# A fused cross-attention, self-attention and 8-bit feed-forward kernel: w_down's rounding and turning moved into the self-attention groups, three banks for gate and up, and two borders reordered

## The reference

```python
x = x + cross_attention(layernorm(x), ctx, Wq, Wk, Wv, Wo, bo)      # 64 x 32 tokens of 512, 257 keys of 384, 16 heads of 64
x = x + self_attention(layernorm(x), Wq, Wk, Wv, Wo, rel_bias_emb)  # per batch of 32 tokens, bias by bucket
x = x + ffn(layernorm(x), clip_x, clip_down, w_gate, w_up, w_down)  # hidden width 1408

def _act_fake_quant(x, clip):                                        # one scale for the whole tensor
    scale = sigmoid(clip) * max(abs(x)) / 127
    return clip(round(x / scale), -128, 127) * scale
def _weight_fake_quant(w):                                           # one scale for each row
    scale = max(abs(w), axis=1, keepdims=True) / 127
    return clip(round(w / scale), -128, 127) * scale
xq = _act_fake_quant(x, clip_x)
h = _act_fake_quant(silu(xq @ wq(w_gate).T) * (xq @ wq(w_up).T), clip_down)
out = h @ wq(w_down).T
```

## Time and profile before

| | us |
|---|---|
| median of 3 runs | 1700.52 (1699.65 to 1701.18) |
| the profiled execution | 1699.84 |
| its span | 1698.1 |
| PE busy | 1602.0 (94%) |
| DVE busy | 1105.7 (65%) |
| ACT busy | 776.6 (46%) |
| POOL busy | 299.0 (18%) |

### The profile page before, as it was taken

How to read it: one execution, slowest core, us unless ns; L and a number is a source line. 1 busy time by engine, 2 the same in 40 slices (tenths; PEclk the granted TensorE clock), 3 DMA queues, 4 the chain that set the end, 5 groups by cost and what they waited for, 6 DMA issues and landing times.

```text
span 1698.1 us, 33888 instructions
## 1 busy us (share of the span) xinstructions
PE 1602.0 (94%) x12487; PEld 1327.5 (78%) x12487; DVE 1105.7 (65%) x2297; ACT 776.6 (46%) x1687; POOL 299.0 (18%) x179
## 2 busy tenths in 40 slices
PE   5999879999999999999999998899999999986888
PEld 4888668898998999989999897778778787763333
DVE  6776666667666766667666676457565565566886
ACT  3555554555545555455554554232122221214555
POOL 0000123222232222323222231100000000002325
PEclk9999989999999999999999999999999999998989
DMA  4898842332133312333123331320202202040032
GB/s 165 324 372 331 321 169 103 114 124 69 73 114 114 124 59 83 114 114 123 48 94 114 114 120 47 102 106 26 100 33 66 85 32 76 33 179 26 32 117 99
DMA packets 68445, 197.82 MB, mean 116 GB/s; under 512 B 4560, under 2 KB 21008, under 8 KB 65552
## 3 DMA queue, kind: packets, MB, share of 16 engines
q1 hardware_dynamic: 68368, 196.73, 31.3%
HBM read 127.77 MB, written 68.94 MB: 116 GB/s over the span
## 4 chain that ended last, share of the span: by engine, by line
PE 61%; issue 28%; DVE 6%; DMA 2%; ACT 2%; POOL 1%; SPq 0%; ACTq 0%; POOLq 0%; DVEq 0%
PE psum_o L641 16%; PE psum_s L610 12%; PE psum_o L656 5%; PE psum_q L669 5%; PE psum_o L522 5%; PE psum_q L610 4%; PE psum_t L621 3%; PE psum_t L581 2%; PE psum_o L1739 2%; PE psum_s L1739 2%; PE psum_q L628 1%; PE psum_t L538 1%; DMA c_raw<-in_ctx_dram 1%; PE psum_q L538 1%; PE psum_s L538 1%
## 5 line engine op out<-in xcount | busy, mean ns | idle before, releaser
L641 PE MATMUL psum_o<-pT,c_nat 128*128 128x512 f32 x1152 | 314.0, 410 | 8.5 <-DVE pT L890 5.2
L610 PE MATMUL psum_s<-cT,qk 128*128 128x258 f32 x1728 | 254.1, 291 | 10.1 <-ACT probs L825 5.3
L610 PEld LDWEIGHTS psum_s<-cT,qk 128*128 128x128 f32 x1728 | 226.9, 191 | 21.4 <-issue 6.2
L641 PEld LDWEIGHTS psum_o<-pT,c_nat 128*128 128x128 f32 x1152 | 207.0, 193 | 45.6 <-DVE pT L890 7.4
L1160 POOL TENSOR_TENSOR c_nat<-c_raw,zero 128x768 fp32r<-128x768 f32 x64 | 95.4, 1491 | 805.7 <-PE psum_o L641 603.4
L825 ACT ACTIVATE probs<-psum_s,nmax 128x257 f32<-128x257 f32 x192 | 91.7, 478 | 222.9 <-DVE nmax L1064 222.7
L1048 DVE SCALAR_TENSOR_TENSOR oT<-p_last,c_last,psum_o 128x512 f32<-128x512 f32 x192 | 142.8, 744 | 72.7 <-PE psum_o L641 70.4
L890 DVE TENSOR_TENSOR pT<-psum_t,pT 128x512 fp32r<-128x512 f32 x128 | 87.7, 686 | 72.5 <-ACT pT L721 72.5
L1163 POOL TENSOR_TENSOR c_nat<-c_raw,c_nat 128x768 fp32r<-128x768 f32 x64 | 122.2, 1910 | 5.0
L721 ACT ACTIVATE cT<-psum_t 128x256 fp32r<-128x256 f32 x192 | 67.3, 388 | 114.4 <-PE psum_t L581 114.3
L1064 DVE TENSOR_REDUCE nmax<-psum_s 128x1 f32<-128x257 f32 x192 | 80.8, 421 | 50.7 <-PE psum_s L610 49.7
(11 more groups left out here) (241 smaller groups left out, 3076.4 us busy)
## 6 DMA issues: line engine op xcount, KB each, us to landing
qk_by_tile<-staged SPq DMA_DIRECT2D x32, 1536.0 KB, 9.9
raw<-qk_by_tile SPq DMA_DIRECT2D x16, 3072.0 KB, 10.6
c_raw<-in_ctx_dram SPq DMA_DIRECT2D x64, 384.0 KB, 3.2
out_dram<-x_out SPq DMA_DIRECT2D x32, 256.0 KB, 2.0
x_in<-in_x_dram SPq DMA_DIRECT2D x4, 1024.0 KB, 5.7
x_res<-in_x_dram SPq DMA_DIRECT2D x16, 256.0 KB, 2.7
x_in<-out_dram SPq DMA_DIRECT2D x4, 1024.0 KB, 7.2
x_res<-out_dram SPq DMA_DIRECT2D x16, 256.0 KB, 2.8
```

Of the source, the lines that this page charges most:

```text
L610: m = pe.matmul(ps[:, 0:SKP], qk[:, part, rg, c, b, :], cT[b % 2][:, moving, c, :], start=(c, part, moving) == (0, 0, 0), stop=(c, part) = ...
L641: i = pe.matmul(ps[:], c_nat[(b - 1) % 2][:, part, k, m * P:(m + 1) * P], pT[:, moving, k, :], start=(k, part, moving) == (0, 0, 0), stop= ...
```

## The change

w_down is prepared like gate/up chunks: chunks 11 to 14 are its four blocks of 128 rows of 1408. There are now 15 chunks, 3, 4, 4, 4 a group, at j = 2, 4, 6, 7, so all of w_down's fall into the last group. The DVE finds scale and clamp (down_scale, filled here), the ACT rounds, the PE transposes 8 and 3 blocks to t1 and t0, the DVE copies, SP stores to wd_dram; wdT is loaded back before wguT. The buffers w_stage, wd_stage, w_nat, wd_nat, w_turned now lie over v2_1, so the ACT waits for the group's last store before it writes v of tile 1 (it waited before aT of tile 0). wdT is [P, KD, FC, P]: a down product reads 512 columns in four runs. From the gate and up turns the steps of w_down are gone on all engines, and the POOL has only the two reductions and the last adds. Gate products use s0, s1, t0, up products o0, o1, t1, with four silu buffers. The row product (ROW) and the sd_wide copy are made before the first turn. At the border to self-attention w2q_low moves ahead of x_out. In the last group: rsqrt of tiles 0 and 1 after x_out of tile 1; aT of tile 3 ahead of the norm of tiles 0 and 1; rsqrt of tile 2; after the last x_out rsqrt of tile 3 and the norm of tiles 2 and 3. w2o_low moves from j = 7 to 6, and turned banks are emptied ahead of the next chunk's scaling. The ACT waits for the last x_out store before it rounds x, since the silu buffers lie over x_out4.

The diff, cut to what the prediction speaks of:

```diff
@@ self_units, gate_up_units, down_units @@
+CHUNK_AT = (2, 4, 6, 7)
-            if j in (3, 5, 7) and (j - 3) // 2 < group_chunks[s]:
-                u.append((("GUT", chunk), "t1"))
+            if j in CHUNK_AT and CHUNK_AT.index(j) < group_chunks[s]:
+                u += [(("GUT", chunk), "t1")] if chunk < 11 else [(("DT", chunk - 11, 0), "t1"), (("DT", chunk - 11, 1), "t0")]
-    u = [((w, i), (("s0", "s1"), ("o0", "o1"))[w == "U"][i % 2]) for i in range(11) for w in "GU"]
-    return u + [(("DT", 0), "t0"), (("DT", 1), "t1")] + (x_units() if not last else [])
+    u = [((w, i), (("s0", "s1", "t0"), ("o0", "o1", "t1"))[w == "U"][i % 3]) for i in range(11) for w in "GU"]
+    return u + (x_units() if not last else [])
...
-        CHUNKS = (2, 3, 3, 3)
+        CHUNKS = (3, 4, 4, 4)
@@ dve_cross_tile @@
                     dve_qk_low(dve, t + 1, 3, section)
+                if not more and b == 3:
+                    dve_weight(dve, "q")
                 if b == 3 and begun:
                     dve_x_out(dve, t, section)
...
-                if not more and b == 3:
-                    dve_weight(dve, "q")
@@ act_self_all @@
                 act_exp(act, s, 0)
+                act.wait_ge(s_wgu, 16 * sum(CHUNKS[:s + 1]))
                 act_self_v(act, s, 1, 0)
...
-                act.wait_ge(s_wgu, 16 * sum(CHUNKS[:s + 1]))
                 act_self_attended(act, s, 0)
@@ dve_gate_up_weights @@
+            if c >= FC:
+                n = c - FC
+                dve.wait_ge(s_down_raw, 16 * n + 16)
+                ch.link(V.tensor_reduce(wrow[:, 0:1], wd_stage[:], AX_X, ALU.max, apply_absolute_value=True))
+                ch.link(V.tensor_scalar(wrow[:, 2:3], wrow[:, 0:1], 1.0 / 127.0, None, ALU.mult))
+                ch.step(V.tensor_scalar(down_scale[:, n:n + 1], wrow[:, 2:3], 1.0, None, ALU.mult))
+                ch.link(V.reciprocal(wrow[:, 4:5], wrow[:, 2:3]))
+                clamp(wd_stage[:], wrow[:, 4:5], wd_stage[:], ch.link).then_inc(s_dclamp, 1)
+                return
@@ dve_self_all @@
                 dve_self_out(dve, s, 1, ch2)
+                if not more:
+                    dve_out_rsqrt(dve, slice(0, 2), ch2)
                 dve_self_attended(dve, s, 2)
...
                 dve_self_out(dve, s, 2, ch2)
+                dve_self_attended(dve, s, 3)
                 if not more:
-                    dve_out_norm(dve, s, slice(0, 3), ch2)
-                dve_self_attended(dve, s, 3)
+                    dve_out_norm(dve, s, slice(0, 2), ch2)
+                    dve_out_rsqrt(dve, slice(2, 3), ch2)
                 dve_self_out(dve, s, 3, ch2)
                 if not more:
-                    dve_out_norm(dve, s, slice(3, 4), ch2)
+                    dve_out_rsqrt(dve, slice(3, 4), ch2)
+                    dve_out_norm(dve, s, slice(2, 4), ch2)
@@ pe_gate_up @@
-                if i == 10:
-
-                    pe.wait_ge(s_dround, n + 1)
...
-                        m.then_inc(done, 1)
@@ pe_ffn @@
-            pe.wait_ge(s_wguback, 16)
+            pe.wait_ge(s_wide, 1)
+            ps, done = empty(pe, U3(("ROW",), 0, "first"))
+            for c in range(KD):
+                m = pe.matmul(ps[:, c * P:(c + 1) * P], sd_wide[:, c, :], ident[:], start=True, stop=True)
+            m.then_inc(done, 1)
+            pe.wait_ge(s_wguback, 32)
...
-                        out_ = pe.matmul(ps[:], hq[n % 2][:, i, m * P:(m + 1) * P], wdT[:, i, :], start=i == 0,
+                        out_ = pe.matmul(ps[:], hq[n % 2][:, i, m * P:(m + 1) * P], wdT[:, :, i, :], start=i == 0,
@@ dve_gate_up @@
-                if i == 0:
-                    dve_down_scales(dve, n, ch)
-                if i == 2:
-                    V.tensor_scalar(wd_stage[:], wd_stage[:], down[:, 2:3], 127.0, ALU.mult, ALU.min).then_inc(s_dclamp, 1)
@@ pool_ffn @@
-            with pool.Fori(0, NCH) as n:
...
-                G.tensor_scalar(wd_nat[:], wd_stage[:], -ROUND, None, ALU.add).then_inc(s_dround, 1)
```

More of the change, by code:

```diff
@@ L863, in act_cross_tile @@
                 act_last_scalars(act, b, 4 * t)
+                if b == 3 and not more:
+                    act_weight(act, "q")
                 if b == 3 and more:
@@ L1363, in pe_turn_weights @@
             pe.wait_ge(s_wround, c + 1)
+            if c >= FC:
+                for part, chunks in enumerate((range(8), range(8, FC))):
+                    ps, done = empty(pe, own(("DT", c - FC, part)))
+                    for k in chunks:
+                        m = pe.transpose(bf16_blocks(ps, 2 * D)[:, k % 8, :], wd_nat[:, k * P:(k + 1) * P], ident16[:])
+                    m.then_inc(done, 1)
+                return
             ps, done = empty(pe, own(("GUT", c)))
@@ L1434, in act_round_weights @@
         def act_round_weights(act, c):
-            act.wait_ge(s_wclamp, 2 * c + 2)
-            if c:
+            if c > FC:
+                for part in range(2):
+                    full(act, own(("DT", c - FC - 1, part)))
+            elif c:
                 full(act, own(("GUT", c - 1)))
-            nc.scalar.activation(w_nat[:], w_stage[:], ACT.Copy, bias=-ROUND).then_inc(s_wround, 1)
+            if c < FC:
+                act.wait_ge(s_wclamp, 2 * c + 2)
+                nc.scalar.activation(w_nat[:], w_stage[:], ACT.Copy, bias=-ROUND).then_inc(s_wround, 1)
+            else:
+                act.wait_ge(s_dclamp, c - FC + 1)
+                nc.scalar.activation(wd_nat[:], wd_stage[:], ACT.Copy, bias=-ROUND).then_inc(s_wround, 1)
         def halves(ap):
@@ L1759, in pe_ffn @@
             pe_gate_up(pe, NCH - 1, "last")
-            pe.wait_ge(s_wide, 1)
-            ps, done = empty(pe, U3(("ROW",), 0, "down"))
-            for c in range(KD):
-                m = pe.matmul(ps[:, c * P:(c + 1) * P], sd_wide[:, c, :], ident[:], start=True, stop=True)
-            m.then_inc(done, 1)
-            for part in range(2):
-                taken(pe, U3(("DT", part), NCH - 1, "last"))
             for n in range(NCH):
@@ L1826, in act_gate_up @@
                 act_x_take(act, 1, n, section, n + 1)
-            for part, chunks in enumerate((slice(0, 8), slice(8, FC))):
-                ps, free = full(act, U3(("DT", part), n, section))
-                act.sem_inc(s_seen, 1)
-                nc.scalar.activation(wdT[:, chunks, bass.ds(n * P, P)],
-                                     bf16_blocks(ps, 2 * D)[:, 0:chunks.stop - chunks.start, :], ACT.Copy).then_inc(free, 1)
         def act_ffn(act):
@@ L1906, in build_kernel @@
         BEFORE_LOOP3 = 6
[L1907 removed]
+        HIDDEN_SCALE_AT = BEFORE_LOOP3 + 2
         def dve_ffn(dve):
```

123 lines of the change are left out of this document (58 added, 65 removed).

## The result

The changed kernel takes **1675.38 us** (median of four runs, 1674.27 to 1676.01), the kernel before 1700.83 (four runs, 1699.65 to 1701.18): ratio 0.9845, 95% interval 0.9831 to 0.9858. The forecast was 1675.5. The profiled execution took 1676.01 with a span of 1674.2, 23.9 less than the 1698.1 of before. Three single runs that took far longer than all others of their kernel (2395.07, 3191.59 and 6631.36 us) are left out of every median and ratio here.

What follows compares the result with a forecast made beforehand. The PE bounds self-attention; elsewhere its waits and fallen clock cost time. Terms -6.8 + 2.3 - 4.5 + 0.1 - 14.8 - 0.9 = -24.6 gave 1675.2 us, 1675.9 on the median, stated as 1675.5; range 1668 to 1685.

Steps and rivals of the forecast that it cites:

- 1, border: Cross- to self-attention border: w2q_low ahead of the x_out add shortens the PE wait (-4.1 us) and keeps its clock (-2.7).
- the bound of -4.1: Border, smaller gain: only the PE wait shortens, by 4.1 us; the clock is not won back.
- 2, self-attention groups: Self-attention: w_down transposes +3.2 us, turned-bank wait gone -1.3, late chunk j = 7 +0.4; sum +2.3, bounds 0 and +10.
- the tight place: Self-attention, chunk j = 7 behind j = 6 with one staging buffer: PE waits 0.3 to 0.4 us, taken as +0.4.
- rival (c): Self-attention chunk loads landing in 12 us instead of 4 make three groups lose time: +29, 1704 us; chance 0.03.
- Rival (b): Self-attention groups lose what the end wins, by +10 us: 1683 us; chance 0.10.
- 3, tail: Last self-attention group: aT ahead of the norm cuts the PE wait, w_down's load delays x_res; -4.5 us, sd_wide copy +0.1.
- 4, gate and up: Gate and up turns: without POOL and w_down steps, with three banks, turns take 23.0, 21.5, 21.5, 19.0 us; -14.8.
- 5, down products: Start of down products: POOL's reduction follows the maximum sooner, without sd_wide copy and POOL loop's end between; -0.9 us.
- Rival (a): Clocks and gaps stay: border -4.1, tail -3.0, gate and up -10; 1684.5 us; chance 0.13.

## Why the prediction was right, term by term

**1, border** (-6.8, measured -6.52): right in both parts. The wait that stays is 1.18 instead of 1.1, and the clock kept its level behind it, which the bound of -4.1 had left open.

**2, self-attention groups** (+2.3, measured +1.76): right. The chunks cost 3.43 (forecast 3.2 + 0.4); the tight place is there at 0.4; what the rest wins is 1.67 where 1.3 was taken. The landing that rival (c) needed did not come near: no PE wait there is over 0.9. Rival (b) falls with it.

**3, tail** (-4.4 with the copy, measured -5.46): mechanism right, size off by 1.1. The mis-sized step is the 1408 KB in SP's queue: taken as 3.5 to 4.6 us, they delayed wguT and xn by 2.5 (14.4 against 11.9, which the trace of before shows for wguT, and 21.2 against 18.7), and the x_res load took 11.1 where it took 8.0. So the PE waited 1.47 instead of 2.4, and the last add came 7.29 after the PE's end ahead of aT, not 8.2. What stands behind the last add is 0.99 longer, forecast 1.2.

**4, gate and up** (-14.8, measured -14.69): right in each turn and in the cause. All PE waits for h and w_down are gone, the copy of x is what is late next. I named three banks beside the missing POOL passes; the runs give the banks nothing where the passes are gone. How much of the late h was the passes' is not fully shown: put back, with two banks, they make the PE wait 3.02 us for h, and in the kernel before these waits were 5.21 (2.20, 1.02 and 1.99). The DVE's own steps on w_down (1.61 and 0.94 a turn) went away too, and no run puts them back by themselves.

**5, down products** (-0.9, measured -0.27): the step itself is right: the reduction's lag fell by 0.9, and the first product starts 1.08 earlier after the last h, 6.35 instead of 7.43. All of that reaches the third block, which starts 23.35 after the first product in both kernels, because the PE waits there for the rounding of h. From there on the profiled execution took 25.37 instead of 24.56, so 0.81 of the 1.08 is gone: the PE waits 2.36 instead of 1.82, the clock falls, the 22 matmuls take 1.68 more, against 0.80 of a later wait saved and 0.07 near the end. What the prediction lacked is this wait and the clock behind it. But the change is not shown to be its cause. The kernel with the late row copy has the same down products, its clock stayed up, and its last h to the end is 54.18, 1.16 less than before; the kernel with the border edit alone has the old down products, its clock fell, and the same stretch is 56.14. Like compared with like, the term is -1.1, and the -0.27 is the side on which one execution fell.

The terms missed by +0.3, -0.5, -1.1, +0.1 and +0.6, and unchanged code by +1.3, so part of the closeness of the sum is luck; the last two of these are a clock that fell in this execution and not in that of before, at places where either can happen. Rival (a) had the right worry at the wrong place: the clock fell behind no gap of the turns, but behind one in the down products that it didn't name.

## What to carry to other kernels

Cut both traces at the same instructions and compare the stretches; gains of 1 us in a 1700 us kernel are seen there and nowhere in the times. When a wait of the bounding engine goes, ask what its successor costs in clock as well as in length: an engine that gets ahead can wait longer later and lose more than it won (in the down products a PE 0.54 ahead lost 0.81), and letting it start on partial data removed that. Whether a clock falls behind a wait can differ between two executions of the same code, so before a loss is put down to a change, look at the same place in other traces. A load put early into a queue "because it is ready" delays every small load behind it; one needed 100 us later belongs behind those that someone waits for.

## What the runs showed of the hardware

**The clock and the length of a wait.** At one and the same place, ahead of the third block of the down products, twelve traces have a wait of the PE for rounded h. Behind waits of 1.71, 1.73, 1.82, 1.98, 1.98 and 1.99 the next 22 matmuls took 4.75; behind 2.15, 2.35, 2.36, 2.38, 2.40 and 2.49 they took 6.43, part of them at the low level. One of each kind:

```profile
1650.73 4.91 PE L1810 MATMUL psum_q<-wdT,hq 128*128 128x512 bf16 x22 [1.98 <-ACT hq L1887]
```

```profile
1647.12 6.59 PE L1811 MATMUL psum_q<-wdT,hq 128*128 128x512 bf16 x22 [2.15 <-ACT hq L1888]
```

(the kernel with the late row copy, and the one with the late load). Two of the rows have 21 records for 22 matmuls, with the same time to the next row. From the start of these matmuls to the end it is 24.47 to 24.57 in the first six and 25.36 to 25.41 in the others, 0.8 more. Old and new down products are on both sides. The rounding of h fixes where the third block starts, so the wait is what the PE has left over, and that depends on how long the clock was low at the start of the down products: six matmuls of the second piece of h took 1.85 to 2.36 where the later wait was short, 1.35 to 1.70 where it was long.

The length of the wait does not decide alone. In the gate and up products of the kernel before, the clock was low behind this one, which rival (a) names (0.61 from 1613.4 to 1616.5):

```profile
1613.38 1.25 PE L1739 MATMUL psum_o<-xqT,wguT 128*128 x4 [1.99 <-DVE h_all L1892]
```

and behind the wait of 2.31 or 2.32 at 31 to 33 us (the two rows below the table), the 24 matmuls took 5.7 in ten of the fourteen traces and 7.3 in four, with untouched code in all.

**The DVE's clamp of x beside a POOL pass.** In the kernel before, the long one ran from 1582.53 to 1586.19, and the POOL:

```profile
1580.69 4.96 POOL L1967 TENSOR_SCALAR wd_stage<-wd_stage 128x1408 f32<-128x1408 f32 x1 [11.65 <-DVE wd_stage L1899]
```

This pass ended at 1585.64, 0.54 before the clamp. With the passes put back, 1571.43 and 1571.97: 0.54 again. The clamp isn't slowed, it is held until the pass is over, and ends the same 0.54 behind it however long it has been waiting (alone it takes 0.68); products with a PSUM input ran at 0.75 beside the same passes. The Trainium skill, SBUF — State Buffer, Who interferes with whom, states just this: whoever issues first has the shared ports for the whole instruction, and the other fully blocks. The trace agrees. By the same rule the prediction weighed 0.8 us for the sd_wide copy; at its new place the reduction starts 0.14 behind the maximum's end while the copy runs, and took 0.44 instead of 0.38. So here the copy cost the reduction 0.06 us at most, and not the 0.8.

**The POOL's loop.** From the end of the last pass in its loop to the reduction behind the loop the POOL took 5.5 to 5.6 us, four times out of four where the reduction was wanted sooner. No row shows what it does in that time, and no run tells the loop's end from a change of instruction.
